# Two VectorE steps moved in an RWKV and mixture-of-experts kernel: the mix for k ahead of an expert tile, the mix for r between the two differences

## What is computed

```
xk = x * mix_k + xx * (1 - mix_k)       # xx: the token before; also xv, xr
k, v, r = xk @ Wk.T, xv @ Wv.T, xr @ Wr.T
...
ww2 = pp + w;  p2 = max(ww2, kk)        # running maximum
e1 = exp(ww2 - p2);  e2 = exp(kk - p2)
aa, bb = e1 * aa + e2 * vv, e1 * bb + e2
...
x = x + (sigmoid(r) * wkv) @ Wo.T
```

## Time and profile before

| what | value |
|---|---|
| median of 3 runs | 947.93 us (945.61 to 949.6) |
| the profiled execution | 952.72 us, its span 950.9 us |
| TensorE busy | 881.5 us, 93% |
| VectorE busy | 846.6 us, 89% |
| ScalarE busy | 740.1 us, 78% |
| GpSimd busy | 231.1 us, 24% |

### The profile page before, as it was taken

How to read it: one execution, slowest core, us unless ns; L and a number is a source line. 1 busy time by engine, 2 the same in 40 slices (tenths; PEclk the granted TensorE clock), 3 DMA queues, 4 the chain that set the end, 5 groups by cost and what they waited for, 6 DMA issues and landing times.

```text
span 950.9 us, 15851 instructions
## 1 busy us (share of the span) xinstructions
PE 881.5 (93%) x4292; PEld 483.4 (51%) x4292; DVE 846.6 (89%) x1533; ACT 740.1 (78%) x1285; POOL 231.1 (24%) x472
## 2 busy tenths in 40 slices
PE   1575999999999999999999999999999999979896
PEld 0242555555555555555555555555555555445444
DVE  4987799999999999999999999999999999967563
ACT  3658688888889888888888888888988888666553
POOL 5451222213131232213122221313123221211100
PEclk9877999999999999999999999999999999999997
DMA  6110000101010010201010010101001010100000
GB/s 216 45 45 1 15 31 1 68 1 67 1 44 22 0 66 0 66 0 57 9 42 24 0 66 0 66 0 44 22 0 66 1 45 1 45 0 24 1 23 22
DMA packets 28789, 29.67 MB, mean 31 GB/s; under 512 B 2106, under 2 KB 28500, under 8 KB 28500
## 3 DMA queue, kind: packets, MB, share of 16 engines
q1 hardware_dynamic: 28756, 29.27, 9.2%
HBM read 20.87 MB, written 8.39 MB: 31 GB/s over the span
## 4 chain that ended last, share of the span: by engine, by line
PE 53%; DVE 25%; issue 13%; ACT 4%; POOL 4%; DVEq 1%; DMA 0%; SPq 0%; ACTq 0%; POOLq 0%
PE pk L451 13%; DVE comb L1408 9%; PE pe L470 6%; PE pe L468 6%; PE pe L469 6%; PE po L537 5%; PE pt L445 3%; PE pe L466 3%; PE pt L665 3%; DVE xr L1172 2%; DVE pp L1219 2%; PE po L511 2%; DVE yo L1183 2%; DVE num L1128 2%; DVE gd L1228 2%
## 5 line engine op out<-in xcount | busy, mean ns | idle before, releaser
L1408 DVE SCALAR_TENSOR_TENSOR comb<-ye,rw,comb 128x256 f32<-128x256 f32 x448 | 214.6, 482 | 19.3 <-ACT comb L786 4.5
L777 ACT ACTIVATE ye<-pe 128x512 f32<-128x512 f32 x256 | 152.2, 595 | 97.8 <-PE pe L470 95.5
L470 PE MATMUL pe<-weh,x1l 128*128 128x512 f16 x512 | 194.0, 379 | 0.0
L469 PE MATMUL pe<-wel,x1h 128*128 128x512 f16 x512 | 194.0, 379 | 0.0
L468 PE MATMUL pe<-weh,x1h 128*128 128x512 f16 x512 | 194.0, 379 | 0.0
L421 POOL TENSOR_TENSOR msv<-ms,rms_eps_c 128x2 f32<-128x2 f32 x32 | 17.4, 545 | 355.0 <-ACT sq L806 355.0
L466 PE MATMUL pe<-brow,ones 128*128 128x512 f16 x256 | 97.0, 379 | 0.0
L392 POOL TENSOR_TENSOR mo<-st 128x4 f32<-128x4 f32 x32 | 11.1, 347 | 338.1 <-DVE st L1192 195.5
L470 PEld LDWEIGHTS pe<-weh,x1l 128*128 128x128 f16 x512 | 50.1, 98 | 60.5
L469 PEld LDWEIGHTS pe<-wel,x1h 128*128 128x128 f16 x512 | 50.0, 98 | 60.5
L468 PEld LDWEIGHTS pe<-weh,x1h 128*128 128x128 f16 x512 | 50.0, 98 | 49.6
(11 more groups left out here) (169 smaller groups left out, 1956.9 us busy)
## 6 DMA issues: line engine op xcount, KB each, us to landing
xa<-in_x SPq DMA_DIRECT2D x16, 512.0 KB, 3.5
xres<-in_x SPq DMA_DIRECT2D x16, 512.0 KB, 4.4
out_y<-yo SPq DMA_DIRECT2D x15, 512.0 KB, 2.9
ye<-in_w_expert SPq DMA_DIRECT2D x2, 1024.0 KB, 8.0
wa<-in_w_attn SPq DMA_DIRECT2D x1, 1024.0 KB, 11.6
out_y<-yo SPq DMA_DIRECT2D x2, 256.0 KB, 2.1
wpw<-in_w_pw SPq DMA_DIRECT2D x1, 256.0 KB, 10.8
wout<-in_w_out SPq DMA_DIRECT2D x1, 256.0 KB, 6.4
```

Source lines behind the costliest of these rows:

```text
L469: nc.tensor.matmul(dst, x1h[:, h, tok], wel[:, h, cols], start=False, stop=False)
L470: mm = nc.tensor.matmul(dst, x1l[:, h, tok], weh[:, h, cols], start=False, stop=h == H - 1)
L777: act.activation(ye[:, i % NY, :], pe[:, i % 2, :], ACT.Silu, scale=1.0 / WSCALE).then_inc(ye_ready.sem, 1)
L1408: v.scalar_tensor_tensor(out=comb[:, t, :], in0=src, scalar=rw[:, t, e:e + 1], in1=comb[:, t, :], op0=ALU.mult, op1=ALU.add).then_inc(comb ...
```

## The change

The two differences become two functions. In the steps with a feed-forward or experts (g or f), the mix of r now stands between them. The mix of k for sequence n moves from behind expert tile 12 to behind tile 11.

```
-                def differences():
+                def difference_fd():
                     dve.wait_ge(p_ready.sem, p_ready.at(a))
 
                     if on(b):
                         dve.wait_ge(wkv.sem, wkv.at(b))
                     v.tensor_tensor(fd[:], pp[:, :, 0:T], pp[:, :, 1:1 + T], ALU.subtract).then_inc(diffs.sem, 1)
+
+                def difference_gd():
                     v.tensor_tensor(gd[:], kk[:], pp[:, :, 1:1 + T], ALU.subtract).then_inc(diffs.sem, 1)
...
                     if on(a):
                         running_maximum()
-                        differences()
+                        difference_fd()
+                        difference_gd()
                         difference_sd()
...
                 if on(a):
                     running_maximum()
-                    differences()
+                    difference_fd()
                     mix(a, 2, xr)
+                    difference_gd()
                 if on(g):
                     scale_h(0)
...
-                            if on(n) and i == 12:
+                            if on(n) and i == 11:
                                 mix(n, 0, xk)
```

## The result

| | before | changed |
|---|---|---|
| median, 7 runs each | 947.93 us (945.61 to 950.57) | 956.77 us (953.09 to 960.03) |
| ratio to before, 95% interval | | 1.0101 [1.0076, 1.0126] |
| the profiled execution, and its span | 952.72 us, 950.9 us | 954.83 us, 953.0 us |

What follows compares the result with a forecast made beforehand. The prediction took VectorE to set the pace, through the chain from gd over GpSimd to hh. 0.69 + 0.12 = 0.81 us over 12.5 steps, less 1.1 us at start-up, gave +9.0 us: 956.9 us, range 946 to 962 us.

Steps and rivals of the forecast that it cites:

- The bound: In the loop, VectorE sets the pace; the chain gd, exponential, squares, GpSimd, hh has no slack left.
- gd's exponential: On ScalarE, the exponential of gd starts 0.83 us late, some 0.04 us after VectorE's result, as r's mix stands ahead.
- hh late by 0.75 us: At VectorE's second scaling, waiting for GpSimd: 0.75 us late a step, chosen near the upper end of 0 to 0.83.
- 0.06 us regained at x: At x on VectorE, bound by aa alone once ScalarE's silu is no longer awaited: 0.06 us off each step.
- 0.12 us for two sums that touch: In VectorE's expert sums, xk no longer hides the latency between experts 1 and 2: 0.12 us longer each step.
- Late at cv by 0.43 us: TensorE's product of cv waits for tr and starts 0.43 us later; VectorE's pace means this is not added.
- The balance of a step: Loop step: 0.69 us from moving r plus 0.12 us from moving xk, 0.81 us longer.
- The start-up: In step g = -1, gd stands behind xr instead of ahead, so everything there is 1.1 us sooner, once.
- The sum: Whole kernel: 12.5 steps of 0.81 us, 10.1 us, less 1.1 us, so +9.0 us, 0.95% slower.
- TensorE sets the pace: Rival: TensorE's two gaps vanish and shorten each step by 0.81 us, to 937 us; 10%.
- GpSimd absorbs the delay: Rival: GpSimd's chain shrinks to its shortest, hh comes about as now, no change, 947.6 us; 13%.
- Lateness adds up: Rival: TensorE's 0.43 us at cv adds to VectorE's loss, 1.24 us a step, to 962.3 us; 7%.

Runs made afterwards that it cites:

- squares_first: The changed kernel with ScalarE doing the squares ahead of gd's exponential instead of behind it; step 54.57 us, one run 949.14 us.
- k11_only: The kernel before with only the mix of k moved from behind tile 12 to behind tile 11; step 54.41 us, median 949.59 us, ratio 1.0017.
- half_r_between: The changed kernel with only the first half of r's mix ahead of gd and the second half behind it; step 54.41 us.
- k_in_tile11: The kernel before with the mix of k moved from behind tile 12 to between the two sums of tile 11; step 54.29 us, one run 947.88 us.
- gd_behind_hh: The changed kernel with the difference gd one place later, behind the first scaling hh; step 55.70 us, one run 969.21 us.
- r_between_only: The kernel before with only the mix of r moved between the differences, k left behind tile 12; step 54.87 us, median 955.05 us, ratio 1.0092.

## Why the prediction was right

**The bound: right.** The step hung on the chain gd, exponential, squares, GpSimd, hh, and TensorE's gaps were not what bound it; squares_first shows the first, k11_only together with the changed kernel the second.

**gd's exponential: right.** Forecast 0.83 us late and some 0.04 us behind gd's end; it is 3.72 - 2.90 = 0.82 us late, and 522.70 is 0.03 us behind gd's end at 522.67.

**hh late by 0.75 us: the mis-sized term.** It measured 0.66 (0.86 - 0.20). The prediction took the GpSimd chain as nearly rigid and chose "near the upper end" between 0 and 0.83. The chain in fact jumps by one convolution instruction of 0.66 us. With msv begun at 5.26 us or, in single steps, up to 5.41 us after fd, hh came at 7.32; with msv at 5.72 or 5.92 it came at 7.98 or later. The boundary lies between 5.41 and 5.72 us: a delay 0.2 us smaller would still have cost a full jump, one 0.5 us smaller nothing, as half_r_between shows for 0.66 us. The sign was thus nearer to going wrong than the 70% said. The Trainium skill, "SBUF — State Buffer", section "Who interferes with whom", has a VectorE instruction with two SBUF inputs contend with a GpSimd instruction that reads SBUF, and one with a single SBUF input not. The prediction worked an estimate of 0.73 us out of it, nearer than the choice by feel, and the way it gave is the measured one: the first operation is held to the end of the third convolution instruction, the second to that of the fourth. The trace agrees with the page: the power is held by the convolution and sd (1.08 and 2.22 us), and not by hh (0.70 us).

**0.06 us regained at x: right**, with 0.02 more that was not forecast (x takes 1.27 us instead of 1.29).

**0.12 us for two sums that touch: right.** k11_only and k_in_tile11 differ by it. The Trainium skill, "VectorE: DVE Perf Modes", section "The DRAIN you can't avoid", found for eight tensor_copy instructions that a semaphore behind each costs nothing extra. That does not carry over to a sum that waits for the one before it: 0.52 against 0.39 us each, and 54.41 against 54.29 us a step.

**TensorE: right.** Late at cv by 0.43 us in the forecast, 0.43 measured (7.28 to 7.71), regained by the router, which is late by what VectorE lost (16.90 to 17.48 us after fd).

**The balance of a step** was 0.75 - 0.06 + 0.12 = 0.81 and came out as 0.66 - 0.06 - 0.02 + 0.12 = 0.70, against 0.71 to 0.72 measured.

**The start-up: too large.** 1.1 us was forecast, 0.5 came (at equal clocks). The step that failed is "everything there is 1.1 us sooner": TensorE's product of r did start sooner (its wait went from 2.40 to 1.26 us), but the product of cv behind it now waits 0.52 us for tr. The same chain that costs time in the loop takes back half the gain here.

**The sum: right by errors that cancel.** +9.0 forecast, +8.8 measured. The steps were put at 10.1 us and came to 8.6, and 0.6 in the tail: the single step was 0.09 us too high (1.1 us in twelve), while the first of the 13, counted by half, costs in full. The start-up was put at 1.1 us and gave 0.5. The two errors, 0.9 and 0.6 us, nearly cancel.

**The rivals.** *TensorE sets the pace* is refuted by k11_only and by the changed kernel itself. *GpSimd absorbs the delay* is false for this change but not as an idea: it does so for gd 0.66 us late. *Lateness adds up* did not occur here; gd_behind_hh, where x waits for silu, shows it 0.8 us further on.

## What to carry to other kernels

Where a step is exactly as long as several loops over different engines, look for the loop that an edit makes longer, before the gap that it closes: a closed gap on the busiest engine (0.38 us a step at k) gave nothing, a chain 0.8 us longer cost 0.66. Where one engine holds another up by whole instructions, such a chain has steps: the first part of a delay can be free and the next cost a full instruction. Before work is moved into an engine's wait, ask what holds the engine waited for: here VectorE's own instructions stretched GpSimd's, and a difference of 1.22 us put into the wait made hh 1.14 us later. And compare a loop's steps, not spans, when an unchanged start-up varies by more than the change is worth.

## What was not expected of the hardware

- A GpSimd power of 128 x 2 numbers takes 0.70 us when VectorE is idle or works on hh, with one input in PSUM, 1.08 beside the convolution and 2.22 when sd follows; it ended some 0.55 us after the VectorE instruction that held it. The short operation ahead of it is held too, so the pair moves by 0.66 us at a time, and once (four steps of r_between_only) hh came another 0.28 us later for the same start.
- The steps of the two profiles of the kernel before agree within 0.02 us or so, while over all twelve profiles what lies ahead of step g = -1 varies from 80.6 to 87.1 us and the tail behind the thirteenth scans from 157.8 to 163.7 us. The kernel before had 87.1 and 86.1 us ahead and 161.2 us behind both times; every other kernel was profiled once, so whether the edits set these two stays open.
- In step g = -1 the product of r took 5.40 us in three of the twelve profiles and 3.70 in the others, and the step 51.6 us where it was 5.40 and 49.4 to 49.9 elsewhere. The granted clock was 0.68 during the long product and 1.00 during the short one; why it fell in some profiles only stays open.
- The eight fp32 matmuls of r took 3.70 us behind a gap or a wait and 3.60 straight behind other matmuls, both at a granted clock of 1.00.
